# Order of a weight load, a table load and a wait in the setup of a two-layer gated transformer

## What is computed

```
x = x + tanh(g_xattn[0]) * attention0(layernorm(x), ctx)   # one head
x = x + tanh(g_ffn[0])   * ffn0(layernorm(x))
x = x + tanh(g_xattn[1]) * attention1(layernorm(x), ctx)   # 16 heads, with Wo
x = x + tanh(g_ffn[1])   * moe(layernorm(x))               # 8 experts, top 2, capacity 512

# ffn0: 1024 hidden, all in steps of 2^-8
h = round8(x @ w1 + b1)
h = round8(gelu as straight lines between 33 points on [-4, 4])
out = round8(h @ w2 + b2)
```

## Time and profile before

| | us |
|---|---|
| three timed runs | 527.77, 529.99, 533.01; median 529.99 |
| the profiled execution | 531.95, of which its span is 530.2 |
| TensorE, VectorE, ScalarE, GpSimd busy | 487.5, 392.7, 263.3, 147.5 |
| mean granted TensorE clock | 0.974 |

### The profile page before, as it was taken

How to read it: one execution, slowest core, us unless ns; L and a number is a source line. 1 busy time by engine, 2 the same in 40 slices (tenths; PEclk the granted TensorE clock), 3 DMA queues, 4 the chain that set the end, 5 groups by cost and what they waited for, 6 DMA issues and landing times.

```text
span 530.2 us, 8669 instructions
## 1 busy us (share of the span) xinstructions
PE 487.5 (92%) x3276; PEld 412.4 (78%) x3276; DVE 392.7 (74%) x750; ACT 263.3 (50%) x413; POOL 147.5 (28%) x124
## 2 busy tenths in 40 slices
PE   6989979998999899899999839899999999999991
PEld 4777669897887687678777625898899999989991
DVE  5796999899997859679779785758576866757441
ACT  3665687776964555365555332335344344434120
POOL 4362200010001113023101205522344628264253
PEclk9999989999999999799999978999999999999997
DMA  6324000000000111212111632114446547472031
GB/s 225 126 50 122 0 2 0 1 1 0 2 1 2 41 41 32 78 52 79 43 50 44 186 80 66 56 21 126 123 105 171 119 131 159 113 156 57 3 42 18
DMA packets 37163, 36.07 MB, mean 68 GB/s; under 512 B 6456, under 2 KB 35970, under 8 KB 36994
## 3 DMA queue, kind: packets, MB, share of 16 engines
q1 hardware_dynamic: 30661, 27.65, 17.0%
q0 software_dynamic: 6144, 7.66, 8.8%
q10 hardware_dynamic: 317, 0.21, 0.1%
HBM read 27.70 MB, written 8.39 MB: 68 GB/s over the span
## 4 chain that ended last, share of the span: by engine, by line
PE 61%; DVE 22%; issue 7%; ACT 3%; SPq 2%; DMA 2%; POOL 1%; ACTq 0%; DVEq 0%; POOLq 0%
PE PS L1409 14%; PE PS L1411 13%; PE PS L1410 13%; PE PS L1800 5%; PE PS L1742 4%; PE PS L1656 3%; DVE tmp L1095 2%; DVE tmp L1082 2%; PE PS L1809 2%; PE PS L1432 2%; DVE hT_lo L1103 2%; SPq L518 2%; DVE st L946 2%; DVE tmp L1070 1%; DVE nmaxC L1126 1%
## 5 line engine op out<-in xcount | busy, mean ns | idle before, releaser
L1409 PE MATMUL PS<-w_hi,hT_hi 128*128 128x256 f32 x384 | 110.8, 288 | 0.2
L1410 PE MATMUL PS<-w_lo,hT_hi 128*128 128x256 f32 x384 | 109.1, 284 | 0.0
L1411 PE MATMUL PS<-w_hi,hT_lo 128*128 128x256 f32 x384 | 109.0, 284 | 0.0
L918 ACT ACTIVATE tmp<-PS,biasT 128x512 f32<-128x512 f32 (+1 forms) x80 | 43.9, 600 | 112.5 <-PE PS L1411 109.1
L651 POOL DMA_INDIRECT out<-tmp,dst_idx x32 | 55.8, 1745 | 99.7 <-DVE tmp L1365 93.0
L1409 PE MATMUL PS<-xT_hi,w_hi 128*128 128x512 f32 (+1 forms) x224 | 81.1, 362 | 0.4 <-DVE xT_lo L970 0.4
L1410 PE MATMUL PS<-xT_lo,w_hi 128*128 128x512 f32 (+1 forms) x224 | 80.7, 360 | 0.0
L1411 PE MATMUL PS<-xT_hi,w_lo 128*128 128x512 f32 (+1 forms) x224 | 80.4, 359 | 0.0
L1409 PEld LDWEIGHTS PS<-w_hi,hT_hi 128*128 128x128 f32 x384 | 74.1, 193 | 3.4 <-issue 2.3
L1410 PEld LDWEIGHTS PS<-w_lo,hT_hi 128*128 128x128 f32 x384 | 74.1, 193 | 0.9
L1411 PEld LDWEIGHTS PS<-w_hi,hT_lo 128*128 128x128 f32 x384 | 74.0, 193 | 0.0
(11 more groups left out here) (241 smaller groups left out, 888.2 us busy)
## 6 DMA issues: line engine op xcount, KB each, us to landing
w_raw<-in_L_ffn_w SPq DMA_DIRECT2D x72, 256.0 KB
residual<-in_x SPq DMA_DIRECT2D x4, 512.0 KB, 5.3
out<-residual SPq DMA_DIRECT2D x3, 512.0 KB, 4.5
normed_rows<-xn SPq DMA_DIRECT2D x3, 512.0 KB, 2.9
kv<-in_L_ffn_b SPq DMA_DIRECT2D x1, 1024.0 KB, 6.8
tmp<-in_L_xattn_Wq SPq DMA_DIRECT2D x2, 256.0 KB, 5.2
out<-residual SPq DMA_DIRECT2D x2, 256.0 KB, 4.3
normed_rows<-xn SPq DMA_DIRECT2D x2, 256.0 KB, 2.4
```

Source lines behind the costliest of these rows:

```text
L918: act.activation(gD[:, G % 2, f, 0:P * n], H[:, G % 2, f, 0:P * n], ACT.Gelu, bias=biasT[:, col:col + 1]).then_inc(e_gelu, 1)
L1409: pe.matmul(o, lh, rh, start=start, stop=False, skip_group_check=skip)
L1410: pe.matmul(o, lh, rl, start=False, stop=False, skip_group_check=skip)
L1411: return pe.matmul(o, ll, rh, start=False, stop=stop, skip_group_check=skip)
```

## The change

Three moves in the setup. On SP, `load_unit(3)` is placed right behind `load_unit(2)`, in front of the twelve placements and their two waits. On ScalarE, the dummy Gelu moves from behind the loop to behind `x_hi(NC)` in the loop's last round. And the wait for all twelve placements leaves VectorE's `quantise(1)` and is now in ScalarE's program, in front of the two Gelus of pair 1.

```
@@ sync
             load_unit(2)
+            load_unit(3)
             sp.wait_ge(v1_copied, 1)
             sp.wait_ge(vblk_zeroed, 1)
             for j, h in PLACES:
                 place_values(j, h)
-            load_unit(3)
             for u in range(PAIRS, 2 * PAIRS + 1):
                 load_unit(u)
@@ scalar, loop over c
                     x_hi(NC)
+                    act.activation(small[:, 20:21], small[:, 16:17], ACT.Gelu)
@@ scalar, in front of the FFN stage
             act.activation(minus_ident, ident[:, :], ACT.Copy, scale=-1.0).then_inc(minus_ready, 1)
-            act.activation(small[:, 20:21], small[:, 16:17], ACT.Gelu)
             to_grid(0)
@@ scalar, loop over g
                         act.wait_ge(quant_ready, g - 1)
+                    if g == 1:
+                        act.wait_ge(v1_placed, 16 * len(PLACES))
                     act.activation(g0B[:, g % 2, :, :], kB[:, g % 2, :, :], ACT.Gelu,
@@ vector, quantise
                 dve.wait_ge(weighted, g + 1)
-                if g == 1:
-                    dve.wait_ge(v1_placed, 16 * len(PLACES))
                 if g >= 2:
```

## The result

| | before | changed |
|---|---|---|
| median of 20 runs each | 532.58 us | 529.15 us |
| ratio, 95% interval | | 0.9955 (0.9936 to 0.9974) |
| profiled execution, its span | 531.95, 530.2 | 529.04, 527.3 |

The kernel is faster by 0.45%, about 2.4 us, where 4.9 us were forecast. The direction is right; the size is half. The ratio compares means; the medians differ by 3.4 us. Of the 4.05 us between the 525.1 us forecast and the 529.15 measured, 2.6 are the starting point: the kernel before has a median of 532.58 us over 20 runs, and the forecast started from 529.99 over three.

A forecast was written before the change was run, and what follows sets the result against it. SP's twelve placements were taken to delay weight unit 3, and so the first FFN pair through ScalarE. 3.6 us of start plus 1.3 us of the dip's return made 4.9 us, giving 525.1 us, range 521.8 to 529.3.

The forecast's parts named there:

- The start: Setup into FFN: unit 3 issued 5.7 us earlier, no wait for its landing, `to_grid(0)` and VectorE's strip 3.6 us sooner.
- no wait on them at the Gelu of pair 1: ScalarE's Gelu of pair 1, at 50.5: last placement lands at 48.9, cost 0; the range keeps 0.8 us.
- The 1.30 us hole at 59.34: TensorE's wait for `x_rest`: it goes, and the block up to the next hole ends at 71.2 instead of 72.48.
- Rival C: Placements issued 5.7 us later hold ScalarE at the second pair; at 12 us landing, 533.4 us; chance 0.06.
- The step that failed: VectorE's `apply(5)` beside GpSimd's split of unit 3: costs 0.5 us, 0 to 0.3 us may leak.
- Rival D: The start comes earlier but the FFN stage gives it back, say by VectorE and GpSimd slowing each other: 529 to 530 us; chance 0.08.
- the dip's return: TensorE after the hole near 72 us: clock stays 1.00 instead of 0.57 over 76 to 80 us; 1.3 us gained.
- a hole of 1.2 us: TensorE's hole near 72 us shrinks from 3.51 to about 1.2 us, and the clock stays 1.00 behind it.

The follow-up runs named there:

- experiment 1: Changed kernel with GpSimd's split of unit 3 held back until group 3's first residual tile is done: ratio 0.9884, median 525.45 us; in a later session 0.988, 525.60 us.
- experiment 2: Changed kernel with only the second half of GpSimd's split of unit 3 held back: apply 2.36 us; one run, 527.51 us.
- experiment 7: Changed kernel with eight unread matmuls before the transposes of FFN pairs 5 and 13: ratio 0.9922, median 527.45 us.
- experiment 5: Changed kernel with the dummy Gelu and its table load back behind the negated identity: ratio 0.9935.
- experiment 3: Kernel of experiment 1 with a GpSimd memset of 128 x 2560 into unused weight space in the split's old place: one run, 525.92 us.
- experiment 8: Kernel of experiment 1 with five unread matmuls at the head of steps 3, 7, 11 and 15 of the second attention: ratio 0.9921, then 0.9922.
- Experiment 6: Kernel before with only the dummy Gelu and its table load moved up: ratio 0.9986.

## Why the prediction was half right

The start held: unit 3's issue (35.20, forecast 35.0), no wait for its landing, `to_grid(0)` 3.6 us sooner, the placements from 36.18 to 46.53, no wait on them at the Gelu of pair 1, whose 0.72 us of idle in the changed kernel were for VectorE's segment; in experiment 1 it started at 50.11, 0.78 us behind the segment, and waited for no placement either. The 1.30 us hole at 59.34 went, and TensorE's block behind it ended at 71.38 (71.2). Rival C did not come about.

**The step that failed** is the one on GpSimd's split beside `apply(5)`: "the nearest row for what that costs is the apply at 28.38 ... 0.5 us, which the 0.6 us gap of VectorE takes in; between 0 and 0.3 us may leak". It measured 1.95 us on the apply, of which 1.35 us leaked (the segment of pair 0 at 46.46 instead of 45.1). The row was the right one; it was read as a price for each apply. It was a price for an overlap of 0.76 us, and the overlap to come was 2.58 us, with the whole cover of VectorE being 0.6 us. Experiments 1 and 2 show it by removal and by dose. The sum had it only as a leak of at most 0.3 us. Rival D, at 0.08, had the right mechanism, with the gain given back almost whole; that its 529 to 530 us hold the measured 529.15 is luck, as the kernel before is 2.6 us slower over 20 runs than the time it was reckoned from.

The second part is the term of 1.3 us for "the dip's return". With VectorE 1.35 us less ahead, the hole in TensorE's order stayed 2.56 us, the clock fell behind it, and the 1.3 us did not come. That the clock holds behind a hole of 1.2 us and that the dip costs over 1 us were both borne out (experiments 1 and 7). But the length of the hole doesn't decide alone: the clock was 0.60 over 74 to 78 us behind 2.20 us (experiment 5) and 0.61 behind 2.56, and 1.00 behind 2.62 (experiment 3). Without the collision the dip was absent in all three profiles (experiments 1 and 8); with it and nothing in TensorE's hole it was there in two and absent in one, so that the collision brings the dip each time is not shown. In sum, at the first residual: 4.9 forecast, less 1.35 us for the collision, less 1.3 for the dip, less 0.2 for the later start of the profile, makes 2.05, and the profiles have 2.12.

That the total, 2.4 us, comes out near this is in part luck. The lead fell to 0.69 us behind the new dip at 130 us, which the prediction did not have, and grew again by the 3.0 us of the dip that is missing in the second attention. Against the kernel before, the version without the collision gains 1.2%, 6.2 us by its ratio (0.9884 and 0.988 in two sessions), more than the 4.9. Counted from `x_hi`, it is 1.34 us ahead of the changed kernel at the segment of pair 1, and 3.86 us at the last FFN residual (174.43 - 37.40 against 178.92 - 38.03): the rest came at the dips near 74 and 130 us. Where the clock dips in the second attention differs even between executions of one kernel: the two profiles of experiment 1's kernel have 0.54 and 1.00 over 212 to 219 us, the changed kernel 1.00 and the kernel before 0.81. I can't split up what is left.

The Trainium skill has the rule that I left out, in "SBUF — State Buffer", section SBUF: two separate sides: VectorE and GpSimd have a shared pair of ports, and it "is an **exclusive lock**, not a bandwidth split"; between a GpSimd instruction and one of VectorE in a two-port mode (or, if GpSimd's reads SBUF, one with two inputs in SBUF), who comes first keeps it for the whole instruction. No trace shows the mode of an instruction. On the hold itself the runs agree: GpSimd's 1.28, 2.58 and 2.32 us held the apply by 0.99, 1.95 and 2.00 us, and the holds end with the GpSimd instruction to within 0.03 us in the two `ve` rows. By that rule, as an estimate, the term would have been the split's 2.58 us less two tiles that get in (1.38 / 4, or 0.35 us each), 1.9 us and not 0.5.

## What to carry to other kernels

A transfer that arrives sooner moves every engine that works on it, not only the one that waited. When work is moved, list what it will lie beside on the other engines, and price the overlap by its length. A row in which an instruction takes far longer than usual and ends together with one of another engine shows such a hold. Here 2.4 us were gained with the collision and 6.2 without it, 1.35 us of the difference as the hold itself and most of the rest at dips of the clock. One wait did it, which puts the GpSimd work beside operations that it didn't hold up (statistics, an operand in PSUM).

## What the runs showed of the hardware that I had not expected

GpSimd work on SBUF stopped some of VectorE's instructions until it was over, instead of slowing them: even a memset of GpSimd did, and even an instruction of VectorE on 128 x 4 elements was stopped (0.17 became 0.73 us). Held were the applies, `ve`, the segment and the cast (0.22 to 0.97 us); not held, beside the split: the residual with an operand in PSUM (1.65 us), the statistics (1.40 us) and a small memset (0.17 us). Experiment 6 has what looks like the reverse, a GpSimd split longer with a VectorE segment inside it (3.08 us and not 2.54).

The best version found is that of experiment 1: 525.5 us where the kernel before has 532.4 in the same session.
